# Expert rows weighed on the way out and added in memory; four buffers of normalised rows; the last expert's weights requested later

## What is computed

```python
x = x + layernorm(attention(layernorm(x), Wq, bq, Wk, bk, Wv, bv, Wo, bo))   # 16 heads of 16
xs = layernorm(x)
dist = sqrt(|xs - centroid|^2)                    # 8 experts
w, sel = top_k(dist, 2);  w = softmax(w)          # two experts a token, and their weights
out = 0
for e in range(8):                                # hidden size 684
    h = silu(xs @ Wg[e] + bg[e]) * (xs @ W1[e] + b1[e])
    out = out + we[:, e:e+1] * (h @ W2[e] + b2[e])    # we: w where e was chosen, else 0
x = x + layernorm(out)
```

## Time and profile before

| | us |
|---|---|
| three timed runs | 1698.15, 1703.57, 1703.62 |
| median | 1703.57 |
| the profiled execution | 1702.11 |
| its span in the profile | 1700.0 |
| normalise stage and routing | about 870 to 1028 |
| expert loop | about 1038 to 1618 |
| from the last scatter's landing to the end | 1621.3 to 1700.0 |

### The profile page before, as it was taken

One profiled execution on the slowest core, in us unless ns is written; L12 is line 12 of the kernel. 1 busy time (PEld: TensorE's weight loads), 2 busy tenths in 40 slices (PEclk: granted clock), 3 DMA queues, 4 the chain that ended last, 5 costly groups with the idle time before them and its releaser, 6 DMA issues.

```text
span 1700.0 us, 31184 instructions
## 1 busy us (share of the span) xinstructions
PE 1496.8 (88%) x9666; PEld 830.6 (49%) x9667; DVE 1192.9 (70%) x1993; ACT 856.6 (50%) x1684; POOL 349.0 (21%) x404
## 2 busy tenths in 40 slices
PE   6887999999999999999997826999999999999900
PEld 3554333333333333333344414777777777777700
DVE  7998989999999999999223583445444454455427
ACT  2333058888888888888863521222222222222226
POOL 5666100000000010001012322222222222222204
PEclk9998579999999999999998757999999999999955
DMA  4474704344453645461428462011001100100072
GB/s 133 137 197 137 149 8 92 61 90 73 68 100 60 128 70 88 67 106 33 136 54 141 154 224 65 31 34 34 31 31 34 34 31 31 36 32 31 28 253 99
DMA packets 115927, 141.97 MB, mean 84 GB/s; under 512 B 52825, under 2 KB 87362, under 8 KB 115842
## 3 DMA queue, kind: packets, MB, share of 16 engines
q1 hardware_dynamic: 109026, 122.21, 31.4%
q0 software_dynamic: 6816, 18.62, 3.4%
HBM read 90.72 MB, written 50.07 MB: 83 GB/s over the span
## 4 chain that ended last, share of the span: by engine, by line
PE 72%; DVE 6%; issue 6%; ACT 3%; SPq 2%; DMA 1%; POOL 1%; DVEq 0%; POOLq 0%; ACTq 0%
PE psum L1532 19%; PE psum L1386 17%; PE psum L1412 15%; PE psum L1551 11%; PE psum L1542 3%; DVE mx L876 2%; PE psum L1398 2%; PE psum L1465 2%; ACT work L1229 1%; SPq L631 1%; ACT weights L1239 1%; PE psum L1463 1%; PE psum L1518 1%; DVE work L1076 1%; PE psum L1484 1%
## 5 line engine op out<-in xcount | busy, mean ns | idle before, releaser
L876 DVE TENSOR_REDUCE mx<-psum 128x1 f32<-128x1024 f32 x512 | 623.4, 1222 | 20.4 <-PE psum L1386 16.9
L1229 ACT ACTIVATE work<-psum 128x512 f32<-128x512 f32 x1024 | 556.7, 597 | 132.2 <-PE psum L1398 69.2
L1386 PE MATMUL psum<-stack 48*128 48x512 f32 x1024 | 394.8, 469 | 7.6 <-DVE mx L876 5.6
L1398 PE MATMUL psum<-stack 50*128 50x512 f32 x1024 | 376.3, 447 | 0.0
L1532 PE MATMUL psum<-weights,values 128*128 x1136 | 341.5, 454 | 0.6 <-DVE values L1095 0.6
L1412 PE MATMUL psum<-work,values 128*32 128x256 f32 x4096 | 328.1, 393 | 9.2 <-ACT weights L1239 9.2
L1386 PEld LDWEIGHTS psum<-stack 48*128 48x128 f32 x1024 | 160.4, 196 | 232.6 <-DVE mx L876 202.3
L1532 PEld LDWEIGHTS psum<-weights,values 128*128 128x128 f32 x1136 | 211.5, 191 | 99.8 <-issue 3.6
L1304 ACT ACTIVATE values<-values 128x342 f32<-128x342 f32 x142 | 69.3, 488 | 257.0 <-DVE values L1105 257.0
L1551 PE MATMUL psum<-weights,work 114*128 (+1 forms) x852 | 195.9, 379 | 0.8 <-ACT work L1314 0.8
L1412 PEld LDWEIGHTS psum<-work,values 128*32 128x32 f32 x4096 | 82.0, 108 | 196.9 <-ACT work L1229 101.6
(11 more groups left out here) (171 smaller groups left out, 1298.5 us busy)
## 6 DMA issues: line engine op xcount, KB each, us to landing
stack<-qk_scr SPq DMA_DIRECT2D x192, 128.0 KB, 6.7
qk_scr<-weights SPq DMA_DIRECT2D x8, 2048.0 KB, 7.1
weights<-in_w SPq DMA_DIRECT2D x8, 1368.0 KB, 6.2
ot_scr<-weights SPq DMA_DIRECT2D x16, 512.0 KB, 3.2
weights<-y_d SPq DMA_DIRECT2D x16, 512.0 KB, 8.7
weights<-in_w SPq DMA_DIRECT2D x8, 684.0 KB
work<-in_b SPq DMA_DIRECT2D x8, 684.0 KB, 6.2
weights<-in_x SPq DMA_DIRECT2D x4, 1024.0 KB, 8.4
```

Source lines behind the costliest of these rows:

```text
L876: dve.tensor_reduce(mx[:, r, a, t:t + 1], bank(4 + 2 * a, 2), AX, ALU.max, negate=True).then_inc(s_max, 1)
L1229: act.activation(pt[u % 4][:, j, :], bank((c + HG * u + n) % 3), ACT.Exp, scale=SC).then_inc(s_exp, 1)
L1386: ins = pe.matmul(bank(4 + 2 * a + half), qs[t3][at:at + QROWS, r, P * t:P * (t + 1)], ks[t3][at:at + QROWS, r, 512 * half:512 * (half + 1 ...
L1398: pe.matmul(bank((t3 + HG * u + n) % 3), ks[t3][at:at + MROWS, r, P * st:P * (st + 1)], qs[t3][at:at + MROWS, r, 512 * half:512 * (half + ...
```

## The change

One row per token is kept in memory instead of two. Ahead of the loop the sums are set to zero by one transfer of 4.3 MB during the second group of attention. The weights `w_1` and `w_2` lie side by side in `w_both`; TensorE transposes them, ScalarE copies the result, and SP stores it as `w_d`, one number for each choice. In the loop a third indirect transfer fetches for each tile the weights of its 128 slots into the column `w_slot`, by the row numbers in `at_w`, which VectorE writes; ScalarE's copy of the result multiplies by it; and the scatter adds to the row of the token. The mixing reads one row per token, has 12 loads, and neither weighs nor adds. The normalised rows have four buffers. The last expert's biases, hitherto loaded with the others, and its weights are requested after the third gather has landed; VectorE waits for them ahead of tile 32, as TensorE does.

```diff
-        xn2 = [c.take([2, C]) for _ in range(2)]
+        xn2 = [c.take([2, C]) for _ in range(4)]
...
+                elif g == 1:
+                    sp.dma_start(y_d.rearrange("(n p) d -> p n d", p=P),
+                                 zeros[:, :].rearrange("p (a d) -> p a d", a=1).to_broadcast([P, NT + 1, C])).then_inc(s_yc, 16)
...
-            sp.wait_ge(s_slot, 1)
+            sp.wait_ge(s_wc, 1)
+            sp.dma_start(w_d[0:2 * NTOK, :].rearrange("(a p) o -> a (p o)", p=P), w_turned).then_inc(s_wd, 16)
+            sp.wait_ge(s_xr, 48)
+            load_b1(sp, E - 1, s_last)
             load_w2(sp, E - 1, s_last)
             load_w1(sp, E - 1, s_last)
...
                 pool.indirect_dma_start(out=y_d, out_offset=bass.IndirectOffsetOnAxis(ap=at_y[:, 0:1], axis=0),
-                                        in_=y_row, in_offset=None).then_inc(s_ys, 16)
+                                        in_=y_row, in_offset=None, compute_op=ALU.add).then_inc(s_ys, 16)
+
+            def gather_weight(t):
+                pool.wait_ge(s_iw, t + 1)
+                after(pool, s_yr, t)
+                settle(pool, passed_pool)
+                pool.indirect_dma_start(out=w_slot[:, :], out_offset=None, in_=w_d,
+                                        in_offset=bass.IndirectOffsetOnAxis(ap=at_w[:, 0:1], axis=0)).then_inc(s_wg, 16)
...
             with pool.Fori(1, NS - 2) as t:
                 gather(t + 2)
                 scatter(t - 1)
+                gather_weight(t)
...
+            def aim_weight(t):
+                after(dve, s_wg, 16 * t)
+                dve.tensor_copy(at_w[:, :], place_of[:, bass.ds(t, 1)]).then_inc(s_iw, 1)
...
+                    aim_gather(t + 2)
+                    aim_scatter(t - 1)
+                    save_ht(t)
+                    aim_weight(t + 1)
...
-                after(act, s_keep[u % 2], 16 * (u // 2))
-                after(act, s_t3, u - 1)
+                after(act, s_keep[u % 4], 16 * (u // 4))
+                after(act, s_t3, u - 3)
...
                 after(act, s_ys, 16 * t)
-                act.activation(y_row, bank(7)[:, 0:C], ACT.Copy).then_inc(s_yr, 1)
+                act.wait_ge(s_wg, 16 * (t + 1))
+                act.activation(y_row, bank(7)[:, 0:C], ACT.Copy, scale=w_slot[:, 0:1]).then_inc(s_yr, 1)
...
-            steps(dve, NT // 2, [(1, mix), (3, invert_mix), (1, stats_mix), (3, offset_mix), (1, means_mix)])
+            steps(dve, NT // 2, [(1, invert_mix), (0, stats_mix), (1, offset_mix), (0, means_mix)])
...
-            steps(act, NT // 2, [(2, deviation_mix), (0, weigh_first), (4, norm_mix)])
+            steps(act, NT // 2, [(0, deviation_mix), (1, norm_mix)])
```

## The result

| | before | after |
|---|---|---|
| median of the timed runs, us | 1701.95 | 1908.28 |
| lowest and highest | 1698.15, 1703.62 | 1896.73, 1911.97 |
| span of the profiled execution | 1700.0 | 1908.0 |

Four runs of each. The ratio of after to before is 1.120, with a 95% interval from 1.115 to 1.126: the change makes the kernel 12% slower. The prediction was 1871 us with a range from 1825 to 1985. The side and the mechanism were right, and the size was 37 us short.

The account below looks back on a forecast made before the run. TensorE was taken to bound the expert loop at 8.07 us a tile, until a new wait chain lengthens it. Sum: 1702.1 + 220 - 22 - 6 + 2 + 1 - 26 = 1871 us, range 1825 to 1985.

Parts of the forecast that it names:

- The ring: Expert loop: VectorE's at_w copy waits for GpSimd's weight fetch, closing a chain of 11.3 us a tile; +220 us over 68 tiles.
- The gap behind the copy to `at_w`: Expert loop, VectorE ahead of a tile's first bias: reading the tile's expert number, taken at 0.36 us.
- The pitch of GpSimd's transfers: Expert loop: start to start of gather, scatter and weight fetch on GpSimd, taken as 1.66 us each.
- the first rival, the slow scatter: Expert loop: the adding scatter also delays the weight fetch, a further +68 to +163 us, 1939 to 2034 us; chance 18%.
- the collision of the last expert's request: First tiles of the expert loop: the moved request for expert 7 delays a fetch there; +2 us, range 0 to +8.
- The rival of the clock: Expert loop: TensorE's granted clock falls in each tile's pause and stays low; up to +549 us, 2200 us; chance 6%.
- The covered ring: Expert loop: the new chain fits in VectorE's slack, tiles stay 8.07 us, only gains remain; 1651 us; chance 6%.
- Four buffers: Normalise stage: ScalarE's waits of 6.99 and 5.78 us for a buffer go; -22 us, range -10 to -24.
- What is late next: Normalise stage: GpSimd's division of the heads' outputs comes late once ScalarE's two pauses go, giving back 1 us each.
- Last expert's weights: Start of the expert loop: the first gather no longer lands behind expert 7's 2 MB request; -6 us.
- The tail: After the last scatter: twelve loads instead of 20 (-11) and no weighing or mixing (-15); -26 us, range -10 to -30.
- The clearing: Second attention group: zeroing the sums, 4.3 MB, some 25 us of DMA beside other work; +1 us, range 0 to +5.

Follow-up runs that it names:

- experiment 1: Changed kernel with VectorE writing at_w for a tile in that same tile, behind at_y, not at the end of the tile before; 1661.3 us, ratio to before 0.979.
- experiment 9: Changed kernel with two at_w columns used in turn, the copy in its old place but waiting for the fetch before the last; 1655.3 us, ratio 0.971.
- experiments 3 and 4: Changed kernel with a second weight fetch into a spare column ahead of the real one: 1982.0 us; the same with at_w written early, in its own tile: 1658.5 us.
- Experiment 10: Changed kernel with the loop's branch and the reading of the expert number moved ahead of the at_w copy that waits; 1831.8 us, ratio to before 1.075.
- experiment 2: Changed kernel with a scatter that does not add, so one of each token's two expert rows is lost; 1855.4 us, ratio to before 1.091.
- experiment 11: Changed kernel with seven more unused products per tile on TensorE, ahead of the transposes of the hidden rows; 1900.7 us, ratio to before 1.116.
- experiment 7: Changed kernel with the last expert's biases and weights requested once the slots are known, as before the change; 1905.0 us, ratio to before 1.118.
- experiment 5: Kernel before with four buffers of normalised rows alone, the last expert's biases requested with its weights at their old place; 1682.6 us, ratio to before 0.990.
- experiment 6: Kernel before with four buffers of normalised rows and the last expert's biases and weights requested after the third gather; 1682.2 us, ratio to before 0.989.

## Why the prediction was right, and where it was short

**The ring is shown, and so is what closes it.** One wait, the protection of a single column, costs 247 us (experiment 1); with a second column it costs nothing although the copy stays where it was (experiment 9); and a further transfer adds its pitch when the ring is closed, and nothing when it is open (experiments 3 and 4).

**Its length, link by link.** The second column adds up to 11.61, the distance measured.

| link | predicted | measured |
|---|---|---|
| end of `at_x` to the gather's start | 0.78 | 0.80 |
| gather's start to scatter's start | 1.66 | 1.26 |
| scatter's start to fetch's start | 1.66 | 1.92 |
| fetch's start to its landing | 2.6 | 2.50 |
| copy to `at_w` and the gap to the first bias | 0.50 | 1.22 |
| first bias to the end of `at_x` | 4.05 | 3.91 |
| tile | 11.25 | 11.61 |

Two links were mis-sized, and in part they cancel. One sum of the prediction is off besides: a tile of 10.8 to 11.9 around 11.25 is 31 us down and 44 up over 68 tiles, not 34 both ways; the measured tile and time lie within either.

The gap behind the copy to `at_w` was taken at 0.36 from the earlier trace rows. That row is the gap between the two halves of one tile. Between two tiles there stand also the loop's branch and the reading of the next tile's number, together 1.07 us. In the kernel before they lay ahead of a wait for TensorE (0.87) and could not be seen; behind a wait that ends last they cost in full. At 1.22 in place of 0.50 the link was short by 0.72 a tile, 49 us over the loop. Experiment 10 shows that it is a link: taken out whole, it gives back 1.0 us a tile, 69 us over the loop. This is the step that failed.

The pitch of GpSimd's transfers was taken at 1.66, from a gap of 0.69 after the gather. With the transfers queued up the gap is 0.30. That is -0.4 for each of two links. On the second the adding scatter, 1.62 us long in place of 0.99, takes its +0.63 back. So the first rival, the slow scatter, came in part: about +50 us (experiment 2), under its lower price of +68. My sum had it at nothing, and the overestimated gaps, 0.8 us a tile or 54 us together, hid that: to this extent the nearness of the sum is luck. Its other part, the longer landing, is not in the ring: the fetch behind a plain scatter lands only 0.1 us sooner. The Trainium skill (DMA: Bandwidth & Descriptors, Rules for kernel authors) says that an accumulating DMA reads its destination and writes it later. The traces agree with a longer way, 3.9 us to landing in place of 2.4, and not with a doubled one.

The Trainium skill's fit for a GpSimd-issued DMA (DMA: Bandwidth & Descriptors, Anatomy of one DMA) gives an estimate of 2.0 us for a fetch of this size; the trace has 2.4 to 2.5, so here the measurement decides against the page by 0.4 us.

In sum the ring took 68 x (11.67 - 8.07) = +245 where the prediction had +220. Of the rest of the loop's +253.9 the collision of the last expert's request is the largest part: the tile that it falls on is 18.8 us long in place of 11.6, +7 where I had +2, and without the collision (experiment 7) this stretch is 5.7 us shorter.

**The rival of the clock** is refuted: the clock did fall, to 0.85 over the tile shown, and filling the pause changed the tile by 0.02 us (experiment 11). The pause covers it, as was argued.

**The covered ring** as a rival named its own price: with no ring in the way, 1651 us. The changed kernel is not that case, but experiments 1 and 9 make it, and measure 1661 and 1655. So the gains are -41 and -47 where the sum had -51, of which the collision that was taken too low is some 4, and all of the change's loss is in the ring.

**Four buffers:** -22 predicted, -22.6 in the stage's trace, -19 in the time of the part alone. The two pauses themselves are 12.8 us of it. The rest is the clock behind them, as the prediction had it: before, TensorE was granted 0.50 from 905 to 915 and from 935 to 950 us, and in the changed kernel 1.00 from 890 to 960. What is late next was also named rightly, the division of heads' outputs on GpSimd (L738), and 1 us each was near. TensorE waits for it twice in the changed kernel, and nowhere in the stage before:

```profile
916.32 0.69 PE L1495 MATMUL psum<-weights,ones_f 1*128 1x256 f32 x2 [1.00 <-POOL weights L738]
936.18 0.69 PE L1495 MATMUL psum<-weights,ones_f 1*128 1x256 f32 x2 [0.64 <-POOL weights L738]
```

The +2.4 in the routing, which the sum did not have, comes with the clock of that execution (experiment 5).

**Last expert's weights:** -6 at the first gather was right, the price of +2 was too small, and in the traces the sum of the two is near zero (experiments 6 and 7). Of the range from 0 to +8 that I gave for the collision nearly the upper end came true, and in the kernel without the ring as well (experiment 6), so it is not the ring that makes it dear.

**The tail:** -26 predicted, -29.9 measured; the loads gave 12.2 in place of 11, the pairs the rest.

**The first stretch**, +10.0, is none of the change's. It arises where the attention begins, at the half clock, before TensorE's granted clock has risen. Before, and after (stretches as above):

```profile
230.00:240.00 10.00, 10.00 (x74) 3.27 (x74) 7.03 (x7) 6.44 (x12) 0.42 (x2) 0.70 0.02 3
240.00:250.00 10.00, 10.00 (x100) 3.64 (x96) 9.96 (x9) 8.76 (x17) 0.00 (x0) 1.00 0.01 2
```

```profile
230.00:240.00 10.00, 10.00 (x58) 3.27 (x60) 6.22 (x7) 5.41 (x11) 0.42 (x2) 0.50 0.02 4
240.00:250.00 10.00, 10.00 (x60) 3.30 (x52) 5.80 (x5) 4.68 (x9) 0.00 (x0) 0.50 0.01 1
```

ScalarE's first copy of a head's output stands at 251.0 before and 260.9 after, and the clearing of the sums is issued only at 308. In the eleven experiments' profiles that copy lies between 249.6 and 261.9: the latest is experiment 5, which has no clearing, and the earliest experiment 7, which has it. So this moment varies by 12 us from one execution to the next. How much of the spread of the times it makes up is not shown: only profiled executions have a trace, and experiment 7's, the earliest at this moment, was still the slowest of its four runs, with the half clock from 880 to 910. What sets it is open. The clearing itself, 4.3 MB that landed in 14.0 us where I had reckoned 25, cannot be seen in the time.

Put together, against the sum's 169: the ring +25, the collision +5, the start +9, the routing +2.4, the tail -4, and 1.5 for the last scatter's own longer landing make 208.

## What to carry to other kernels

An index column, or any small buffer, that an in-order engine may overwrite only when a transfer has landed ties that engine to the transfer's whole chain. Ask who is queued behind the wait, and give it a second column or move the write to where the transfer has long landed; here the second column turned +12% into -3%. When a ring is added up, every link between two waits counts, with the loop's branch and the register loads, and the gap must be read at that very place in the program, not at a similar one. A transfer moved away from one critical place has gained nothing until the place that it moves to has been checked for somebody who waits.

## What the runs showed of the hardware

- An indirect scatter of 128 rows of 1 KB with addition takes GpSimd 1.62 us in place of 0.99, and 3.9 us to land in place of 2.4.
- An indirect fetch of 128 numbers of 4 bytes lands in 2.4 us, as long as 128 rows of 1 KB scattered without addition.
- Indirect transfers that are queued up on GpSimd start 0.30 us after the end of the one ahead. The 0.69 us of the earlier trace rows were not its least gap.
- TensorE's granted clock fell to 0.85 over a tile with a pause of 3.8 us and was 1.00 when the pause was filled, with no effect on a tile that the ring sets.
- The moment at which the clock rises at the start of the attention varied between executions: ScalarE's first copy of a head's output came at 249.6 to 261.9 us.
- At the end of the normalise stage TensorE was granted 0.52 to 0.59 in six executions and 0.94 to 1.00 in six others with the same code there; the same eight products took 3.62 us (experiment 5) and 1.91 us (experiment 1).
